# Two routing groups of 9 and 7 pairs in place of three of 7, 5 and 4, in a transformer block with a mixture of experts

## What is computed

```python
mod = (silu(c) @ wmod).reshape(32, 6, 1, 128)
sa, ca, ga, sb, cb, gb = mod[:, 0], ..., mod[:, 5]      # ga, gb are kept away from 0
h = layernorm(x) * (1 + ca) + sa
x = x + ga * attention(h)        # linear attention: elu+1 features, causal, 32 wide, with a memory term
h = layernorm(x) * (1 + cb) + sb
gate = softmax(h @ w_gate.T)                 # 8 experts
scores, idx = top_k(gate, 2)                 # each token goes to 2 of them
y = gelu(h @ W1[e] + b1[e]) @ W2[e] + b2[e]  # 128 -> 512 -> 128
x = x + gb * sum(scores * y)
```

## Time and profile before

| what | us |
|---|---|
| median of 3 runs | 572.16 (571.8 to 572.68) |
| the profiled execution | 572.52 |
| its span in the trace | 570.8 |
| PE busy (matmul) | 382.1 (67%) |
| DVE busy | 450.4 (79%) |
| ACT busy | 331.5 (58%) |
| POOL busy | 312.9 (55%) |

### The profile page before, as it was taken

The page is one execution under the profiler, slowest core; times in us unless marked ns, Lnnn a source line. Parts: engine busy times, 40 slices in busy tenths (PEclk is TensorE's granted clock), DMA queues, the critical chain, the costliest instruction groups (busy, mean ns, idle before and its releaser), DMA issues.

```text
span 570.8 us, 14921 instructions
## 1 busy us (share of the span) xinstructions
PE 382.1 (67%) x4184; PEld 339.5 (59%) x4185; DVE 450.4 (79%) x1081; ACT 331.5 (58%) x746; POOL 312.9 (55%) x344
## 2 busy tenths in 40 slices
PE   3551646874377646626999999999999999930000
PEld 3341545764276535514998999999898898930000
DVE  4659888888888888755888888988999999975213
ACT  1432547896188836424666667767666666694211
POOL 2248200000277777777777500077878878788671
PEclk9997768788587876856999999999999999985555
DMA  3499101526154751812474433455555555566231
GB/s 108 130 316 358 39 1 32 164 73 196 41 165 133 234 155 52 233 55 79 115 147 138 130 99 95 100 130 143 129 143 133 133 134 137 123 172 168 60 84 53
DMA packets 129681, 73.19 MB, mean 128 GB/s; under 512 B 53745, under 2 KB 122993, under 8 KB 129393
## 3 DMA queue, kind: packets, MB, share of 16 engines
q1 hardware_dynamic: 121456, 56.02, 35.3%
q0 software_dynamic: 8192, 16.79, 11.1%
HBM read 21.75 MB, written 34.90 MB: 99 GB/s over the span
## 4 chain that ended last, share of the span: by engine, by line
PE 39%; DVE 27%; POOL 14%; issue 10%; ACT 4%; DMA 3%; DVEq 2%; ACTq 0%; SPq 0%
PE psA L1149 16%; POOL ROW L493 14%; PE psA L1137 8%; PE psV L1137 4%; PE psH L1137 4%; DVE ATT L747 3%; PE psH L1047 3%; DVE X L816 2%; DMA X<-in_x 2%; DVE stats L690 2%; DVE stats L823 2%; DVE w_bound L926 2%; ACT HH L580 1%; ACT ATT L574 1%; DVE AM L778 1%
## 5 line engine op out<-in xcount | busy, mean ns | idle before, releaser
L482 POOL DMA_INDIRECT slot_rows<-ROW,POS x128 | 132.4, 1034 | 114.3 <-DVE EXPT L901 75.9
L493 POOL DMA_INDIRECT ROW<-slot_out,POS x128 | 147.0, 1148 | 86.6 <-DMA slot_out<-VP 48.1
L1149 PE MATMUL psA<-WST,ATT 128*128 x2040 | 139.1, 221 | 2.0 <-DVE VP L970 1.6
L1149 PEld LDWEIGHTS psA<-WST,ATT 128*128 128x128 f16 x2040 | 125.0, 98 | 12.3 <-issue 3.6
L961 DVE SCALAR_TENSOR_TENSOR ATT<-ATT,f_scales 128x1024 f16<-128x1024 f32 x85 | 109.1, 1284 | 3.0
L635 ACT ACTIVATE ATT<-psA,b1T,f_scales 128x256 f32<-128x256 f32 x172 | 83.1, 563 | 36.0 <-PE psA L1137 35.2
L959 DVE TENSOR_SCALAR ATT<-ATT,f_scales 128x1024 f16<-128x1024 f32 x85 | 65.2, 768 | 22.6 <-ACT ATT L635 21.2
L1137 PE MATMUL psA<-WT,WST 128*128 128x256 f16 x516 | 65.7, 279 | 5.9 <-DVE RT L889 3.7
L635 ACT ACTIVATE ATT<-psV,b1T,f_scales 128x256 f32<-128x256 f32 x84 | 42.9, 561 | 37.1 <-PE psH L1137 33.2
L1137 PEld LDWEIGHTS psA<-WT,WST 128*128 x516 | 48.4, 99 | 13.9 <-issue 6.6
L1047 PE MATMUL psH<-ident,ATT 128*128 128x128 f32 x64 | 15.2, 380 | 57.7 <-DVE ATT L747 57.7
(11 more groups left out here) (200 smaller groups left out, 721.5 us busy)
## 6 DMA issues: line engine op xcount, KB each, us to landing
slot_out<-VP SPq DMA_DIRECT2D x85, 128.0 KB
slot_rows<-zero SPq DMA_DIRECT2D x9, 1024.0 KB, 5.8
X<-in_x SPq DMA_DIRECT2D x8, 512.0 KB, 7.8
WST<-in_W SPq DMA_DIRECT2D x2, 2048.0 KB, 11.8
WST<-WT SPq DMA_DIRECT2D x16, 256.0 KB, 2.3
out<-X SPq DMA_DIRECT2D x16, 256.0 KB, 2.4
slot_rows<-ROW,POS POOLq DMA_INDIRECT x128
GA<-gate_rows SPq DMA_DIRECT2D x1, 2048.0 KB, 11.4
```

Source lines behind the costliest of these rows:

```text
L482: nc.gpsimd.indirect_dma_start(xg[g], bass.IndirectOffsetOnAxis(ap=POS[:, k * TILES + t:k * TILES + t + 1], axis=0), ROW[:, t * 2 * D:(t + ...
L493: nc.gpsimd.indirect_dma_start(YG[:, o:o + D], None, yg[g], bass.IndirectOffsetOnAxis(ap=POS[:, i:i + 1], axis=0)).then_inc(gathered[c % 2 ...
L1149: last = mm(psD[k % 2][:, h * D:(h + 1) * D], a[:, k % 2, i:i + TOK], W2S[:, ds(e * 2 * FF + b * FF + m * D, D)], start=(m == 0 and c == 0 ...
```

## The change

`GPAIRS` becomes (9, 7). Everything that is computed from it follows: two groups of 36 and 28 tiles with 43 and 35 slots, 78 in all; 72 and 56 scatters; `MIX0` goes from 6 to 7 and `MIXED` from 4 to 2. In `steps`, the loops now cover steps 5 to 8, 9 and 10, 11 and 12, 13 and 14, with route 0 behind step 10 and the other route behind step 17. The slices of the weights are converted in the same steps as before.

```diff
-    GPAIRS = (7, 5, 4)
+    GPAIRS = (9, 7)
...
-            for g, (first, end) in enumerate(((2, 4), (4, 6))):
+            for first, end, n_of in ((2, 4, 0), (4, 5, 1), (5, 6, 1), (6, 7, None)):
                 with eng.Fori(first, end) as n:
                     for k in range(2):
-                        step(2 * n + 1 + k, 1 - k, n + k, **({"weights": (g, 2 * n - 4 + k)} if weights else {}))
-                if g == 0:
-                    route(g)
-            for p in range(PAIRS - 3, PAIRS + 2):
+                        step(2 * n + 1 + k, 1 - k, n + k, **({"weights": (n_of, 2 * n - 4 + k)} if weights and n_of is not None else {}))
+                if end == 5:
+                    route(0)
+            for p in range(PAIRS - 1, PAIRS + 2):
                 step(p, p % 2, p // 2)
-                if p == PAIRS_TO[1] + 1:
-                    route(1)
             last()
             route(GROUPS - 1)
```

## The result

The changed kernel takes 604.88 us (median of 4, 603.82 to 605.38) against 571.98 for the kernel before (median of 4, 570.68 to 572.68). The ratio is 1.0575, with a 95% interval from 1.0551 to 1.06: slower by 5.8%, about 33 us. The profiled execution took 603.82 with a span of 602.1, so 31.3 us more span than before. The forecast was 607, with a range of 595 to 614.

A forecast was written before the change was run, and what follows sets the result against it. Handovers between stages were taken to set the end, POOL's issue time the tail. Span 570.8 + 14.3 (scatter) + 2 (broadcast) + 22.4 (larger first group) − 4.5 (gathers) = 605.0, plus 1.72: 606.7, said as 607 us, range 595 to 614.

The forecast's parts named there:

- What bounds the kernel: Whole kernel: handovers between stages set the end; in the tail POOL's own issue time is the bound.
- Slots: Expert stage: 78 slots for 85 save 19.4 us there, but 8 more in the first group delay the gathers 22.4 us.
- Routing and steps: DVE in attention: route 0 of 36 tiles takes some 15.5 us, from 159.8 to 175.3, behind steps 9 and 10.
- Scatter 0: POOL before the expert stage: 72 scatters use up about 30 us of slack; first up matmul at 274.5, +14.3 us.
- The broadcast: SP's 2,048 KB load into GA, now beside the expert stage's start, delays slot 4: +2 us, bounds 0 and 11.4.
- the restart: PE at the expert stage's start: ±3 us in the range for starting after a longer idle stretch, clock granted at 0.67.
- When the gathers start: POOL's first gather: 371.50 + 14.3 + 2 + 22.4 = 410.2, 38.7 us later.
- Gathers: POOL's 128 gathers: 28 more run beside an idle PE and DVE, gaining 0.161 each, −4.5 us; bounds nothing or 6.7.
- The free price: POOL's gathers after the expert stage ends: 1.318 us each, against 1.479 while it runs.
- The collision of transfers: Rival, DMA at the expert stage's start: slot 4 loses the full 11.4 us, 616.1 us in all; chance 0.13.
- The scatter gates: Rival claimed scatter 0 does not gate: expert stage follows attention at 254, end 583.9 us; chance 0.04.
- POOL's issue price: Rival: POOL's price is congestion, falling to 1.05 us a scatter and 1.24 a gather, 562.1 us; chance 0.02.

The follow-up runs named there:

- e5: The kernel before with 36 memsets on POOL, about 20 us, ahead of group 0's first scatter: 573.66 us (ratio 1.0034).
- e7: The changed kernel with three groups of 9, 4 and 3 pairs, 85 slots, and a route added behind step 14: 608.69 us (ratio 1.0636).
- e4: The changed kernel with 16 of group 0's 72 scatters left out: 585.95 us (ratio 1.0238).
- e6: The changed kernel with 36 memsets on POOL, about 20 us, ahead of group 0's first scatter: 625.29 us (ratio 1.0919).
- e1: The changed kernel with SP's 2,048 KB broadcast into GA issued ahead of the first slot load: 600.81 us (ratio 1.0509).
- e3: The changed kernel with groups of 7 and 9 pairs, route 0 where the kernel before has it: 602.37 us (ratio 1.0527).
- e2: The changed kernel with groups of 8 and 8 pairs, route 0 behind step 9: 591.37 us (ratio 1.0323).

## Why the prediction was right, and where it was off

**What bounds the kernel.** Right. The gathers begin on the first group's last output and then run on POOL without a pause; e5 and e7 show both halves of it. Two readings were off without weight in the sum. Counted from slice 1, POOL's blocks are slices 12 to 22 and 27 to 39, and PE is at 9 in slices 20 to 35. And the chain's 14% for POOL, from which the prediction took that the end is set by handovers, leaves out the first 56 gathers, as shown above.

**Slots.** Right: 78, and the stage itself ends 5 us earlier although it starts 12 later. e7 shows what that saving was worth in the whole, 4 us. The 8 more slots ahead of the gathers come to 22.4 as taken, at an unchanged pace.

**Routing and steps.** Route 0 took 15.6 us (15.5 worked out) and ended at 174.2 (175.3). It began at 158.57 where 159.8 was worked out, and 1.0 of these 1.2 us lies in the two steps ahead of it, which took 20.6 in place of 21.6 from the first mask product on. That is the lower bound that stood beside them (two steps of 10.19 are in fact 1.3 less than 21.7, not 1.2). The added loops cost nothing that can be seen.

**Scatter 0.** Forecast +14.3, measured +11.7 (271.94 − 260.24). The steps give 1.1 of the difference, the scatters 1.0 (1.290 each instead of 1.304), the release of SP and the landing 0.5. That this term is on the path at all was the main claim, and e4 and e6 show it from both sides: 18.9 us for 20.6 taken away, 20.4 for 21 added.

**The broadcast.** This term was mis-sized, the mechanism was right. Forecast +2; in the trace slot 42 comes 3.4 us later behind slot 0 than by the usual pace (405.86 − 285.11 = 120.8, against 42 × 2.795 = 117.4), and e1 puts the whole at 4.5. The load was late as worked out: the broadcast took 12.4 us here in place of 11.4, so it landed at 287.5, and PE went on at 288.02. The Trainium skill ("DMA: Bandwidth & Descriptors", "Queues, rings and completion order") says that on each DMA engine the descriptors of one issuer's ring are consumed in ring order; the trace agrees, with slot 4's matmuls 0.5 us behind the landing, and e1 with the wait gone. What the term left out is the slower PE after the hole: it was granted 0.61 and 0.53 of the clock in the 4 us behind it, and its next 36 matmuls took 1.7 us longer than in e1. The range had ±3 for the restart, but the sum had nothing.

**When the gathers start.** 410.2 forecast, 409.14 measured. That it fits so well is in part luck: the stage began 2.6 us too early for the forecast, and from its first matmul to the first gather it took 137.2 us where 111.3 + 22.4 + 2 = 135.7 was worked out, 1.5 more.

**Gathers.** Forecast −4.5, measured −6.8. The free price held, (588.96 − 556.76 − 1.85)/23 = 1.320 against 1.318. Beside the expert stage a gather cost 1.456 (the first 64, to 502.34) rather than 1.479, 1.5 us of the difference. The total lies just past the bound of 6.7 that the prediction gave. Which work makes them dearer there was not tried.

**The rivals.** The collision of transfers was there, at 4.5 us of the 11.4 it could have cost, inside the forecast's case. The scatter gates, as said. POOL's issue price did not fall as that rival had it: 71 spacings of scatters cost 1.290 with fewer routings beside them, where it needed 1.05, and the gathers cost 1.320 even behind the expert stage, where it needed 1.24.

In the theories for the experiments two things were missing: that the second group's scatters can gate its first slot, and with it the last two slots of the group ahead of it (e3), and that the mixing's place moves in steps of 8 slots (e2). The first was dismissed rightly for the changed kernel only, where slot 43 was not loaded until some 45 us after the last scatter at 345.04.

## What to carry to other kernels

In a pipeline of stages over groups, fewer groups save their padding, but the first group's size is paid in full before the next stage can begin, and the last group's after the one before it has ended; a saving inside a stage that bounds neither is worth little (19 us of work for 4 here). Before a producer is moved later, look how long its result has been lying ready, here 30 us, and which transfers were parked in that slack: they collide with the start once it is gone.

## What the runs showed that was not expected

A wait of PE in the expert stage cost more than itself, twice. A broadcast of 2,048 KB in front of a slot's load cost 4.5 us with a wait of 2.7; the granted clock was 0.61 and 0.53 in the 4 us behind the hole, and 1.00 without it. In e2 a wait of 3.3 us of DVE, which held PE up for 3.5, made its turn of 8 slots 5.5 longer; there the granted clock was 0.50 from 406 to 412.

Executions of kernels with the same attention code up to step 8 reach that step at different times: 127.21 to 131.90 among the eleven profiled ones. In e7 the 3.5 us were still there at the first gather, 4.0 later than in the changed kernel. So a single trace is compared from a common point, as the first up matmul in e1, rather than by its absolute times. Where the attention stage loses them was not looked into.
